# Graph and bit-linear block: held copies of the first block-product item moved ahead of the last h rows, and ternary weight sets dealt out anew

## The reference, cut to what matters

```python
h   = relu(xn @ Wself0 + deg_inv * (A @ xn) @ Wneigh0 + b0)     # first edge stage: sum over A
gnn = h @ Wself1 + deg_inv * (A @ h) @ Wneigh1 + b1             # block products, second edge stage
x1  = x + gnn + mix(xn)                                         # mix: linear attention
out = x1 + bitlinear(gelu(bitlinear(layernorm(x1), w1)), w2)
bitlinear: round(a * 127/max|a|) @ clip(round(w / mean|w|), -1, 1)
```

## Time and profile before

| what | us |
|---|---|
| median of three runs | 1330.73 |
| profiled execution | 1337.23 |
| its span, first to last instruction | 1335.4 |
| PE busy | 1296.3 (97%) |
| DVE (VectorE) busy | 835.1 (63%) |
| ACT (ScalarE) busy | 662.2 (50%) |
| POOL busy | 99.2 (7%) |

### The profile page before, as it was taken

One profiled execution on the slowest core, in us unless ns is written; L12 is line 12 of the kernel. 1 busy time (PEld: TensorE's weight loads), 2 busy tenths in 40 slices (PEclk: granted clock), 3 DMA queues, 4 the chain that ended last, 5 costly groups with the idle time before them and its releaser, 6 DMA issues.

```text
span 1335.4 us, 18779 instructions
## 1 busy us (share of the span) xinstructions
PE 1296.3 (97%) x6370; PEld 615.7 (46%) x6370; DVE 835.1 (63%) x1464; ACT 662.2 (50%) x905; POOL 99.2 (7%) x94
## 2 busy tenths in 40 slices
PE   9999999999999999999999969999999699999999
PEld 5454444555445444444444424444444244444444
DVE  7854541453668778949964643444658668886774
ACT  7775655345122355524424743846833267474460
POOL 0000000000000002100000101432322100000000
PEclk9999999999999999999999989999999999999999
DMA  8488896855045457526876998798568718823523
GB/s 346 150 280 283 265 278 210 305 208 174 0 174 187 151 200 234 177 92 230 284 234 187 243 287 224 205 317 290 174 224 282 217 50 242 203 72 99 127 49 109
DMA packets 203093, 269.10 MB, mean 202 GB/s; under 512 B 110464, under 2 KB 144000, under 8 KB 199424
## 3 DMA queue, kind: packets, MB, share of 16 engines
q1 hardware_dynamic: 190432, 255.93, 60.8%
q10 hardware_dynamic: 11136, 6.82, 2.3%
q0 software_dynamic: 1440, 5.24, 2.1%
HBM read 184.33 MB, written 57.67 MB: 181 GB/s over the span
## 4 chain that ended last, share of the span: by engine, by line
PE 83%; DVE 7%; DMA 6%; SPq 2%; issue 1%; ACT 1%; DVEq 0%; ACTq 0%
PE ps L2246 36%; PE ps L2568 12%; PE ps L2377 8%; PE ps L2670 8%; PE ps L2527 7%; PE ps L2633 7%; PE ps L2446 2%; DMA S<-HL 1%; DMA Zb<-blocks_scratch 1%; DMA S<-SPLIT 1%; PE ps L2385 1%; PE ps L2298 1%; DVE TMP L1972 1%; DVE HL L1993 1%; PE ps L2280 1%
## 5 line engine op out<-in xcount | busy, mean ns | idle before, releaser
L2246 PE MATMUL ps<-S,XH 128*128 128x512 f16 x1440 | 317.1, 379 | 0.6 <-DVE Zb L1672 0.6
L2246 PEld LDWEIGHTS ps<-S,XH 128*128 128x128 f16 x1440 | 139.9, 98 | 165.5 <-DVE Zb L1672 3.0
L2246 PE MATMUL ps<-S,Zb 128*128 128x512 f16 x480 | 106.4, 379 | 0.0
L2377 PE MATMUL ps<-XH,S 128*128 128x512 f16 (+1 forms) x576 | 102.6, 339 | 0.0
L2246 PE MATMUL ps<-Zb,XH 128*128 128x512 f16 x432 | 94.8, 379 | 0.0
L2527 PE MATMUL ps<-XH,AT 128*128 128x512 f16 x400 | 86.8, 379 | 2.4 <-DVE TMP L1972 2.4
L1013 ACT ACTIVATE AT<-ps 128x320 f16<-128x320 f32 x40 | 17.4, 434 | 142.4 <-PE ps L2246 142.3
L2527 PE MATMUL ps<-Zb,AT 128*128 128x512 f16 x400 | 86.5, 379 | 0.0
L1625 DVE TENSOR_SCALAR STREAM<-tables,keys 128x320 f16 x240 | 71.2, 297 | 24.3 <-PE ps L2446 14.5
L2377 PEld LDWEIGHTS ps<-XH,S 128*128 128x128 f16 x576 | 56.1, 98 | 47.0 <-issue 2.3
L2246 PEld LDWEIGHTS ps<-S,Zb 128*128 128x128 f16 x480 | 46.9, 98 | 54.4 <-issue 0.6
(11 more groups left out here) (316 smaller groups left out, 2000.8 us busy)
## 6 DMA issues: line engine op xcount, KB each, us to landing
STREAM<-in_w_all SPq DMA_DIRECT2D x48, 512.0 KB, 4.9
STREAM<-in_w1t SPq DMA_DIRECT2D x44, 512.0 KB, 5.0
STREAM<-in_w2t SPq DMA_DIRECT2D x28, 512.0 KB, 5.0
XIN<-in_x SPq DMA_DIRECT2D x20, 512.0 KB, 5.1
Zb<-in_w1t SPq DMA_DIRECT2D x14, 512.0 KB, 7.3
blocks_scratch<-S SPq DMA_DIRECT2D x4, 1792.0 KB, 8.6
blocks_scratch<-STREAM SPq DMA_DIRECT2D x4, 1792.0 KB, 8.6
S<-blocks_scratch SPq DMA_DIRECT2D x7, 1024.0 KB, 10.4
```

Source lines behind the costliest of these rows:

```text
L2246: last = mm(acc[:, n * BANK:(n + 1) * BANK], left(l, kc), right(kc, r)[:, n * BANK:(n + 1) * BANK], start=(kc == 0 and i == 0), stop=(kc = ...
L2377: last = mm(ps[:, 3 * j * BANK + a:3 * j * BANK + b], Wq_s[:, kc, l, mc], XH[:, r, kc, a:b], start=(kc == 0 and l == 0 and r == 0), stop=( ...
```

## The change

- In `h_act(p)` the L1118 copy (with its wait for `h_turned1`) moves behind the square; for the last pair all three `st_copy(0, 0..2)` stand between the square and that copy. `st_act(0)` is no longer called.
- VectorE's low parts split off as `h_lows(p)`, called at once for pairs 0 to 3; for pair 4 it stands behind `c11(0)` and `c22(0)`.
- SP issues `h_turn_left` and `h_turn_rest` ahead of a set's load and store.
- Sets: 3 instead of 4 in `H_QUADS`; items get 0, 2, 3, 2, 0, 2, 3, 3, 3, 3 (before 0, 1, 3, 3, 0, 2, 2, 2, 3, 2); one (31) in the second edge stage, made like the others.
- The third set of items 6 to 9 (`CLIPPED`) has no relus on ScalarE; VectorE clips the raw rows in one more pass over 128 x 2048 f32 and then subtracts MAGIC.

```diff
-EDGE_QUADS = 11
-LAST_QUADS = 29
+EDGE_QUADS = 10
+LAST_QUADS = 31
-        H_QUADS = {t: EARLY_QUADS + t // 2 for t in range(1, NT - 2, 2)}
-        ST_COUNTS = (0, 1, 3, 3, 0, 2, 2, 2, 3, 2)
+        H_QUADS = {t: EARLY_QUADS + t // 2 for t in range(1, NT - 4, 2)}
+        ST_COUNTS = (0, 2, 3, 2, 0, 2, 3, 3, 3, 3)
-        X1_QUADS = {0: 29, 1: 30, 3: 31}
+        CLIPPED = [quads[2] for quads in ST_QUADS[PAIRS:] if len(quads) > 2]
+        X1_QUADS = {1: 31}
...
@@ sync, first edge stage
+                    if t == 2 * p:
+                        h_turn_left(p)
+                    elif p < PAIRS - 1:
+                        h_turn_rest(p)
                     if t - 1 in H_QUADS:
                         i = H_QUADS[t - 1]
                         quad_load(i + 1)
                         quad_store(i)
-                    if t == 2 * p:
-                        h_turn_left(p)
-                    elif p < PAIRS - 1:
-                        h_turn_rest(p)
...
@@ scalar, h_act
-                    else:
-                        wait(act, "h_turned1", 64 * p)
-                        A(HL[:, 1, 0, BANK:D], TMP[:, 1, BANK:D], ACT.Copy).then_inc(S("h_hi"), 1)
                     A(banks(4), TMP[:, j, :], ACT.Square, accum_out=at("h_sq", t)).then_inc(S("h_sq"), 1)
                 if p == PAIRS - 1:
                     act.wait_ge(S("c_x"), 1)
-                    st_copy(0, 0)
+                    for which in range(3):
+                        st_copy(0, which)
+                wait(act, "h_turned1", 64 * p)
+                A(HL[:, 1, 0, BANK:D], TMP[:, 1, BANK:D], ACT.Copy).then_inc(S("h_hi"), 1)
...
@@ scalar, st_act
-                cuts = {1: (2, 2, 2, 2, 4, 4)}.get(i, (2, 4, 5, 6, 10, 12))
+                cuts = (2, 2, 2, 2, 4, 8) if i == 1 else (2, 4, 5, 6, 8, 12)
...
@@ vector, quad
+                if i in CLIPPED:
+                    link(V.tensor_scalar(raw_rows, raw_rows, MAGIC - 1.0, MAGIC + 1.0, ALU.max, ALU.min))
+                    V.tensor_scalar(made[:, 0:4, :], raw_rows, -MAGIC, None, ALU.add, saturate=False).then_inc(S("made"), 1)
...
@@ vector
-            st_dve(0)
+            c11(0)
+            c22(0)
+            h_lows(PAIRS - 1)
+            c12(0)
+            c21(0)
```

More of the change, by code:

```diff
@@ L632, in _ @@
             sp.wait_ge(S("z1_lo"), 3 * PAIRS)
-            for n in range(2):
-                quad_load(LAST_QUADS + n)
+            for n in range(LAST_QUADS, N_QUADS):
+                quad_load(n)
             for b in range(2):
@@ L661, in _ @@
                 x2T_turn(t, t % 2)
[L662 to L666, removed]
+                if t - 2 in X1_QUADS:
+                    quad_store(X1_QUADS[t - 2])
             def hid_turn(t, half, product):
@@ L787, in _ @@
                         .then_inc(S(f"s1_out{p % 2}"), 16)
[L788 to L793, removed]
+            for i in range(ST_QUADS[PAIRS][0], N_QUADS):
                 last_blocks(i)
[L796 to L799, removed]
         @block.scalar
@@ L1046, in quad_round @@
                     act.wait_ge(pieces_in(i, n), 16 * quad_nth(i) + 32 if quad_at(i) < 4 else 32 * quad_nth(i) + 32)
-                    A(piece, piece, ACT.Identity, bias=col("magic"), scale=col("isw")[:, w:w + 1]).then_inc(S("rounded"), 1)
+                    A(piece, piece, ACT.Identity, bias=col("magic"), scale=col("isw")[:, w:w + 1])\
+                        .then_inc(S("rounded"), 2 if i in CLIPPED else 1)
                 else:
@@ L1155, in st_act @@
             def st_act(i):
-                rounds = [later_round(k, part) for k in ST_QUADS[i] for part in range(4)]
-                cuts = {1: (2, 2, 2, 2, 4, 4)}.get(i, (2, 4, 5, 6, 10, 12))
+                rounds = [later_round(k, part) for k in ST_QUADS[i] for part in range(2 if k in CLIPPED else 4)]
+                cuts = (2, 2, 2, 2, 4, 8) if i == 1 else (2, 4, 5, 6, 8, 12)
                 def some(n):
@@ L1166, in st_act @@
                 t = 2 * (j - PAIRS)
-                if i > 0:
-                    st_copy(i, 0)
+                st_copy(i, 0)
                 some(0)
@@ L1183, in st_act @@
                 some(5)
-            st_act(0)
             norm("norm_h", 1, 6)
@@ L1208, in _ @@
                 y_round(t)
-                if t in X1_QUADS:
-                    for part in range(4):
-                        quad_round(X1_QUADS[t], part)
+                for part in {0: (0, 1), 1: (2, 3)}.get(t, ()):
+                    quad_round(LAST_QUADS, part)
             for b in range(2):
@@ L1712, in source_sum, with quad @@
                                 AXX, ALU.add).then_inc(S("added"), 1)
-            def quad(i, both=True):
+            def quad(i):
                 made = blocks_made(i)
@@ L1718, in quad @@
                 wait(dve, f"made_out{i % 2}", 16 * (i // 2))
-                if i > LAST_QUADS:
-                    dve.wait_ge(S("made"), 2 * i)
                 dve.wait_ge(S("rounded"), 4 * i + 4)
[L1722 to L1725, removed]
+                if i in CLIPPED:
+                    link(V.tensor_scalar(raw_rows, raw_rows, MAGIC - 1.0, MAGIC + 1.0, ALU.max, ALU.min))
+                    V.tensor_scalar(made[:, 0:4, :], raw_rows, -MAGIC, None, ALU.add, saturate=False).then_inc(S("made"), 1)
+                else:
+                    V.tensor_scalar(made[:, 0:4, :], raw_rows, 2.0, -1.0, ALU.min, ALU.add,
+                                    saturate=False).then_inc(S("made"), 1)
                 dve.wait_ge(S("made"), 2 * i + 1)
@@ L1830, in h_sums, with h_lows @@
                 V.tensor_tensor(S4_, A12, S2_, ALU.subtract).then_inc(S("h_sums"), 1)
+            def h_lows(p):
+                A22 = TMP[:, 1, BANK:D]
                 dve.wait_ge(S("h_hi"), 4 * p + 2)
@@ L1849, in _ @@
                 h_sums(p)
+                if p < PAIRS - 1:
+                    h_lows(p)
             def row_half(i, row, half):
@@ L2027, in _ @@
                 if t - 1 in X1_QUADS:
-                    quad(X1_QUADS[t - 1], both=False)
+                    quad(X1_QUADS[t - 1])
                 if t == 3:
```

1 line of the change is left out of this document (added).

## The result

The changed kernel takes 1312.76 us (median, 1312.00 to 1315.21) where the kernel before took 1330.55 beside it: ratio 0.9869, 95% interval 0.9847 to 0.9891. I had predicted 1300, with 1293 to 1305 for the forecast itself and 1292 to 1313 for the whole range. The direction holds, but about 13 us of the gain are missing. The median lies at the range's edge, and by the ratio (0.9869 of the 1330.73 that I had started from) it is 1313.3, just past it. The profiled execution takes 1312.0 us (span 1310.2), 25.2 less than the profiled one of before.

What follows compares the result with a forecast made beforehand. PE was taken as the bound, with four waits that matter. Terms 15.2 + 16.2 + 1 - 1 - 0.5 - 0.3 = 30.6 us took the profiled 1337.23 to 1306.6; 6.5 less for the median gave 1300, range 1292 to 1313.

Steps and rivals of the forecast that it cites:

- Term (1): Item 0's copies first: PE's 12.51 us wait before P6 and the slow clock behind it go, gain 15.2 us.
- Term (3): Sets in items 1 to 3: new stall 0 to 4 us, taken as 1; the block wait shrinks, taken as -1.
- The step from the profile to the median: Whole kernel: the runs' median is 6.5 us below the profiled execution, so 1306.6 becomes 1300.1, said as 1300.
- (5): Second edge stage with one set: waits of 2.4, 0.5, 11.92 us and 1.4 of slow clock go, 16.2 together, less 0.3.
- (2): SP's new order, transposes ahead of a set's load and store: taken as 0, bounds -1 and +12 us.
- (4): Three sets in items 6 to 9 with a clipping pass on VectorE: cost 0 to 2 us, taken as 0.5.
- rival C: Port lock: each clipped pass waits 1.7 us for POOL in items 6 to 9, 5 us lost, 1305; chance 0.10.
- Rival A: Waits return: set transfers late in items 2 and 3 (to 4 us) and 6 to 9, 7 us lost, 1307; chance 0.16.
- B: Item 0: tile 9's s0 row or T1 caught by block loads, only 16.2 us come, 1314.5; chance 0.09.
- D: Items 6 to 9: set loads take 20 us and PE stands before P6 and P5, slower at 1338; chance 0.05.

Runs made afterwards that it cites:

- e2: Kernel before with only the order of item 0's copies changed (`h_act`, `h_lows`), sets and SP order as before: 1330.14 us, ratio 0.9985.
- e1: Kernel before, unchanged, run again for a second profile: 1331.82 us, ratio 0.9985.
- e15: Changed kernel with item 0's accumulating DMAs held until the last transposes land, and loads of sets 11 to 16 cut to 64 columns: 1304.58 us, ratio 0.9792.
- e4: Changed kernel with item 0's two accumulating DMAs held until the last transposes have landed: 1312.92 us, ratio 0.9844.
- e18: Changed kernel again, nothing altered: 1314.82 us, ratio 0.9866.
- e10: Changed kernel with the loads of sets 11 to 16 cut to 64 of 1024 columns (values not the reference's): 1307.07 us, ratio 0.9812.
- e3: Changed kernel with the new order of item 0's copies undone, its sets and SP order kept: 1319.18 us, ratio 0.9894.
- e13: Changed kernel with SP's order of before, transposes and stores of h behind a set's load and store: 1312.23 us, ratio 0.9858.
- e8: Changed kernel with `CLIPPED` empty, so ScalarE does all four parts of the third set: 1315.86 us, ratio 0.9875.
- e9: Changed kernel with the four block loads issued by SP behind the last pair's first transposes, not from ScalarE's queue: 1315.59 us, ratio 0.9883.

## Why the prediction was wrong, by its own steps

- **Term (1), item 0's wait: its mechanism and its size in the trace were right, its worth was not.** 15.5 us came at P1 of item 1, against 15.2. But e2 shows the part alone to be worth nothing measurable. In it the first set load went out at 819.29, and 4.7 us of waits came back behind it; and in e1, which has no long wait in item 0, there was less to take away than in the execution that I had read. I had asked what was late next and looked at the blocks and ScalarE, not at who else would start earlier.
- **Term (3) is the first of two steps that failed.** I took 1 us of stall (0 to 4) and 1 us back. Measured: 9.7 us of waits and what came with them, and 2.0 back, 7.7 lost on balance; e15 says 8 to 10. Two errors. I let the first set load go out "perhaps at 811"; it went out at 818.46, since making item 0 faster released its accumulates 15 us earlier, onto the last transposes (e4 shows this part: 812.70 when they are held). And I took landings of 5 to 8.7 us for all sets, from two places. Sets 11 and 12 landed in 5.6 and 8.6 us, but from set 13 on, with stores, accumulates and a block due in 15 us less time, they take 10 to 11 in the median (up to 12.9 in e4 and 12.6 in e18); e10 shows what this part costs. I had also named set 13 as the tightest, and it was set 11.
- **The step from the profile to the median is the second.** I took 6.5 us off for the median, as if the profiled execution were slow everywhere alike. Set beside e1 (1332.2 us) it was slow in the items alone, 200.1 us against 194.0, where it had the 12.5 us wait, which the change removes. That this holds for the other executions is argued from two traces; in e3, where nothing waits behind it, the execution with the long wait (1316.9) was below that kernel's median. The changed kernel's profile (1312.0) lies 0.8 us *below* its median. So of 12.8 us of error, 25.2 measured against 30.6 in the sum are 5.4 (7.7 lost in term (3), less 2.3 that came elsewhere above the sum), and the conversion is the other 7.3 (6.5 + 0.8). e15 checks this: with term (3)'s cause taken away, its profiled execution is at 1304.7, 32.5 us below that of before, where the sum had 30.6. So the sum's gain was there to be had from the execution that I had read, and the time is still 1304.6 and not 1300.
- **Terms (5), (2), (4)** were right: 16.8 us against 15.9; 0 (e13); 0 against 0.5 (e8), with no wait of PE in items 6 to 8 and in item 9 only the 0.8 us of before. The port lock of rival C showed in the passes (0.8 us an item), not in the time.
- **Rival A** is what happened, in its first half (items 2 and 3 up to 4 us), but starting with the set of item 1, and larger. Its second half, items 6 to 9, did not occur, nor did B or D.

That plain loads on another queue slow a transpose is shown by e9 against the changed kernel (5.7 and 16.0 us for the second S<-SPLIT), and that accumulates do by e4 (3.8 and 4.1 us against 6.5 and 11.6). The Trainium skill (DMA: Bandwidth & Descriptors, "Queues, rings and completion order") says that each DMA engine goes round between the queue rows packet by packet. The trace agrees. While both queues had work, in the changed kernel's DMA view of 786 to 796 us, ScalarE's (q10, the blocks) and SP's (q1, the transposes) sent nearly the same number of packets, but 3.48 MB against 0.12 (packets, MB, share of the engines):

```profile
q10 hardware_dynamic: 473, 3.48, 95.5%
q1 hardware_dynamic: 478, 0.12, 7.3%
```

In the kernel before it is 420 packets to 425 from 787 to 796 us. Taking turns by packets, a queue of 0.25 KB packets gets almost nothing beside one of 7.4 KB packets: from 784 to 800 us the transposes need 4033 of them.

## What to carry to other kernels

When a wait is removed, list every DMA whose issue hangs on the work that now ends earlier, also on other engines' queues, and ask which transfers they will meet: here two accumulates moved 15 us forward onto the transposes that gated the next loads. Before a wait is put into a sum, look for it in a second execution: a wait that comes from two transfers meeting within 2 us may be there in one and replaced by another in the next, as between the two traces of the kernel before. And take the gain from the same execution as the wait; don't carry that execution's excess over the median to the kernel that no longer has the wait.

## What was not expected of the hardware

- The landing of a small transpose depends on its neighbours: some 4 us for one of S<-SPLIT with no other queue busy, 6.5 and 11.6 beside two accumulates, up to 16.0 beside four 1 MB loads.
- SP is held while it issues a transpose into busy queues: 3.35 to 3.41 us for two in a quiet stretch, 9.42 beside the accumulates, 13.94 beside the blocks (3.62 for the same two in e9). What stands behind on SP is late with it: the set loads at 818.46 instead of the 812.70 of e4.
- Short waits cost clock too. Behind 4.42 us the granted clock was 0.66 and then 0.77. Of 13 waits between 2.59 and 3.48 us in the items of these runs, 10 had a first group of 12 matmuls of 4.07 to 5.30 us behind them instead of 2.75; behind those of 2.5 us and less there was none. Over the 13 this is 1.2 us each on average, so a wait of 3 us costs some 4.2.
